# Three 16-wide attentions as one packed, one-pass score program, with the clip moved to the exponentials

## The chip, the cores and the metric

One core of a Trainium2 chip runs the whole kernel in one launch. The metric is the device time of that launch in microseconds (us). TensorE is called PE in the rows, VectorE DVE, ScalarE ACT, GpSimd POOL and SyncE SP.

## The reference

Eight residual blocks act on `x` (8 batches × 256 rows × 256); each takes a layernorm of `x` and adds its result times tanh of a gate. The context is 8 × 256 × 192. Three blocks matter here; each has 16 heads of width 16.

```python
# l1x: cross attention; masked query rows attend evenly
attn = jnp.einsum('bhnd,bhmd->bhnm', q * scale, k)
attn = jnp.where(pad_mask[:, None, :, None], attn, jnp.float32(-1000000000.0))
out = jnp.einsum('bhnm,bhmd->bhnd', softmax(attn), v)
# l3x: cross attention with biases, clip and projection
attn = jnp.einsum('bhqd,bhkd->bhqk', q, k) * scale
attn = jnp.clip(attn, -CLAMP, CLAMP)                       # CLAMP = 10000.0
x = jnp.einsum('bhqk,bhkd->bqhd', softmax(attn), v).reshape(B, Nq, Cq)
return x @ Wo + bo
# l3f: self attention; 5 register rows, the others split in pos and ~pos
l = jnp.where(key_mask[:, None, None, :], logits, -jnp.inf)   # registers + same side
reg_out = (x_pos[:, :REG] + x_neg[:, :REG]) * 0.5
tok_out = jnp.where(pos[:, :, None, None], x_pos[:, REG:], x_neg[:, REG:])
return out @ W_proj + b_proj
```

The other blocks are a similarity (l0x), a feed-forward block (l0f), two mixtures of experts (l1f, l2f) and an attention with heads of width 64 (l2x).

## The kernel before

The blocks run one behind the other with a barrier of semaphores (`phase`) between them. Each engine has its own instruction stream, written out in Python; the order in which the code emits instructions is the order on the engine, and engines meet through semaphores alone. Nothing reorders them.

Two programs compute 16-wide heads.

**Packed** (class `Packed`, function `packing` for each engine) serves l1x. GpSimd splits q, k, the layernormed x and the context into a high part in the fp32r format and a low part (`parts`: a cast, L717, and a subtraction, L719). Products run as three one-pass products of parts (`mm3`, L1736 to L1738). SyncE copies the parts of q and k by DMA (`rows_of`, L563) into `qpack` and `kpack`, so that 48 rows hold (high, low, high) of q against (high, high, low) of k for one head: a single pass of 48 rows then gives the score with little loss. A head needs two sets of scores: queries × keys (L2091), of which VectorE takes the negated maximum (`maximum`, L1163), and keys × queries (L2105) with two more rows that add the negated maximum. VectorE splits the maxima (`maxima`), PE transposes them (L2074), ScalarE copies them out and SyncE writes them to `qpack`. ScalarE's exponential (L1629) then writes the probabilities already transposed, and PE multiplies them with the values of four heads at a time (`values`, L2120). A column of ones beside the values gives the sum.

In loop round n, PE does the first scores of batch n+1 beside the transposed ones of batch n, since these use different halves of the rows; between heads stand the transposes and products that prepare batch n+2 and finish batch n−1. PSUM has eight banks: two for scores, two for transposed scores, two for probabilities × values, and two "rooms" (banks 6 and 7) that everything else takes in turn (`place`). VectorE's round: the maxima, the mask multiply at head 4, both halves of the outputs at head 8.

**Attn** serves l2x, l3x and l3f. Heads of 16 are padded to 32 columns and scored in fp32 (L1898). In l3x VectorE clips every score (L1042) and takes the maximum (L1044); ScalarE's exponential has the maximum as a bias. PE transposes the probabilities (L1915), ScalarE (l3x) or VectorE (l3f) copies them out of PSUM, PE multiplies with the values (L1939) and projects (`finish`: transposes L1982, products L1987). The loop over batches is a hardware loop in which the projections stand between two batches. GpSimd does one root a batch (L700). l3f also scores 80 register queries (5 rows × 16 heads) and keeps pos and neg apart by two mask rows in q and k.

## Time and profile before

| what | us |
|---|---|
| three timed runs, median (lowest to highest) | 3416.39 (3400.31 to 3434.22) |
| profiled execution, its span | 3390.0 |
| l1x, from 263.4 to 538.0 | 274.6 |
| l3x, from 2334.5 to 2799.0 | 464.5 |
| l3f, from 2870.3 to 3382.0 | 511.7 |

For the profiled execution only its span is given: the time from its first to its last instruction. The stages' limits are the barriers between blocks, read from the timeline. Times of instructions below come from that one execution.

### The profile page before, as it was taken

The page shows a single profiled execution, that of the slowest core. Times are in us where ns is not written, and L with a number is a line of the kernel's source. Part 1 is how long each engine was busy: PE and PEld are TensorE (multiplying, and loading weights), DVE is VectorE, ACT ScalarE, POOL GpSimd, SP SyncE. Part 2 cuts the span into 40 slices and gives each one's busy share as a digit, 9 for nine tenths or more (in the row PEclk, how much of TensorE's full clock was granted, in tenths as well). Part 3 has the DMA queues.
Part 4 walks back from the last instruction along what each step waited for, and adds up shares of the span by engine and source line. Part 5 has one row for each costly group of instructions (what it writes and reads, how often), then busy time and mean ns, then how long its engine had stood idle before and what let it go on. Part 6 is the DMA issues. An engine that isn't in the chain of part 4 may idle for free.

```text
span 3390.0 us, 37402 instructions
## 1 busy us (share of the span) xinstructions
PE 2575.8 (76%) x13142; PEld 1918.9 (57%) x13142; DVE 1580.7 (47%) x2934; ACT 872.7 (26%) x2012; POOL 785.2 (23%) x709
## 2 busy tenths in 40 slices
PE   3795885487887728888888577673888884999998
PEld 3574554376666625555556466552555653766665
DVE  3443566256657423333334533224564554454454
ACT  1221342111111103323333112122453451232232
POOL 3103223334334133333434422213000000000000
PEclk8795676699898868888989588786896996988899
DMA  3704441122232230000000013321000000000000
GB/s 115 253 0 57 56 60 54 68 96 98 78 103 91 83 118 5 2 2 2 2 2 0 13 50 95 105 86 55 5 3 2 5 1 0 1 0 0 0 0 25
DMA packets 91147, 151.93 MB, mean 45 GB/s; under 512 B 7612, under 2 KB 75900, under 8 KB 88428
## 3 DMA queue, kind: packets, MB, share of 16 engines
q1 hardware_dynamic: 61820, 101.93, 11.1%
q0 software_dynamic: 8736, 27.76, 2.6%
q10 hardware_dynamic: 20496, 20.97, 1.7%
q8 instruction: 59, 0.97, 0.1%
q14 instruction: 36, 0.29, 0.0%
HBM read 90.51 MB, written 47.19 MB: 41 GB/s over the span
## 4 chain that ended last, share of the span: by engine, by line
PE 57%; issue 20%; DVE 10%; POOL 5%; DMA 3%; ACT 3%; SPq 1%; another core or an unknown queue 1%; ACTq 0%; DVEq 0%; POOLq 0%
PE bank L1898 11%; PE bank L1853 7%; PE bank L1736 6%; PE bank L1915 6%; PE bank L1737 5%; PE bank L1738 5%; PE bank L1939 4%; PE bank L1873 2%; DMA arena<-rows_by_expert 2%; POOL arena L786 2%; DVE nmax L1044 1%; PE bank L1987 1%; DVE split L1332 1%; PE bank L2091 1%; ACT arena L1457 1%
## 5 line engine op out<-in xcount | busy, mean ns | idle before, releaser
L1898 PE MATMUL bank<-arena 64*128 64x256 f32 x1536 | 472.4, 442 | 6.2 <-ACT arena L1457 6.2
L1898 PEld LDWEIGHTS bank<-arena 64*128 64x128 f32 x1536 | 283.0, 207 | 141.6 <-issue 108.5
L1542 ACT ACTIVATE arena<-bank,nmax 128x256 f32<-128x256 f32 x512 | 226.3, 470 | 459.8 <-DVE nmax L1044 457.8
L1915 PE MATMUL bank<-ident,arena 128*128 128x128 f32 x1536 | 272.0, 306 | 74.7 <-POOL arena L829 44.2
L1044 DVE TENSOR_REDUCE nmax<-bank 128x2 f32<-128x512 f32 x256 | 175.8, 690 | 321.0 <-PE bank L1898 316.9
L1457 ACT ACTIVATE arena<-bank 128x512 f32<-128x512 f32 (+1 forms) x346 | 198.2, 580 | 463.1 <-PE bank L1853 112.0
L1736 PE MATMUL bank<-split,ewl 128*128 128x512 f32 x514 | 227.3, 442 | 98.8 <-DVE arena L1329 86.2
L1915 PEld LDWEIGHTS bank<-ident,arena 128*128 128x128 f32 x1536 | 177.6, 151 | 210.1 <-issue 112.2
L700 POOL TENSOR_TENSOR rstd<-rstd,mhalf 128x2 f32<-128x2 f32 x40 | 28.0, 700 | 996.8 <-DVE rstd L972 839.2
L1329 DVE TENSOR_TENSOR arena<-sil,bank 128x512 f32<-128x512 f32 x136 | 93.2, 685 | 315.9 <-ACT sil L1670 300.3
L1737 PE MATMUL bank<-split,ewh 128*128 128x512 f32 x514 | 217.2, 423 | 0.0
L1738 PE MATMUL bank<-split,ewh 128*128 128x512 f32 x514 | 215.5, 419 | 0.0
L1333 DVE TENSOR_TENSOR split<-arena,split 128x512 fp32r<-128x512 f32 x136 | 211.9, 1558 | 4.7
L759 POOL CAST ewh<-ew 128x1536 fp32r<-128x1536 f32 (+1 forms) x47 | 91.6, 1948 | 500.0 <-DMA ew<-in_we 500.0
L761 POOL TENSOR_TENSOR ewl<-ew,ewh 128x1536 fp32r<-128x1536 f32 (+1 forms) x47 | 204.2, 4344 | 3.8
L1054 DVE COPY arena<-bank 128x512 f32<-128x512 f32 (+1 forms) x264 | 177.1, 674 | 55.7 <-PE bank L1915 55.6
L1670 ACT ACTIVATE sil<-bank 128x512 f32<-128x512 f32 x136 | 81.4, 598 | 440.5 <-PE bank L1738 413.6
L1736 PEld LDWEIGHTS bank<-split,ewl 128*128 128x128 f32 x514 | 107.9, 210 | 131.5 <-DVE arena L1329 71.5
L1736 PE MATMUL bank<-ewh,split 128*128 128x256 f32 x544 | 167.8, 309 | 17.7 <-DVE split L1333 10.0
L1939 PE MATMUL bank<-arena 128*17 128x256 f32 (+1 forms) x1536 | 157.3, 423 | 24.2 <-ACT arena L1457 16.6
L825 POOL TENSOR_TENSOR esum<-esum,minus 128x2 f32<-128x2 f32 x128 | 89.8, 702 | 326.8 <-ACT arena L1542 326.7
L1737 PE MATMUL bank<-ewl,split 128*128 128x256 f32 x544 | 155.8, 286 | 0.0
(394 smaller groups left out, 4764.7 us busy)
## 6 DMA issues: line engine op xcount, KB each, us to landing
ew<-in_we SPq DMA_DIRECT2D x32, 768.0 KB, 8.0
ew<-in_we SPq DMA_DIRECT2D x15, 1408.0 KB, 6.1
rows_by_expert<-mrow ACTq DMA_DIRECT2D x1, 20480.0 KB, 58.2
arena<-rows_by_expert SPq DMA_DIRECT2D x23, 512.0 KB, 6.5
rows_by_expert<-arena SPq DMA_DIRECT2D x38, 256.0 KB, 5.4
ct<-in_ctxT SPq DMA_DIRECT2D x32, 192.0 KB, 2.4
kpack<-khl SPq DMA_DIRECT2D x48, 128.0 KB, 4.4
qpack<-qhl SPq DMA_DIRECT2D x48, 128.0 KB, 5.8
```

What stands on the lines that cost most here:

```text
L761: nc.gpsimd.tensor_tensor(low, whole, high, ALU.subtract).then_inc(m["ws"], 1)
L1044: V.tensor_reduce(nmax[:, h, :], src.rearrange("p (t k) -> p t k", t=T), AXX, ALU.max, negate=True).then_inc(m["mx"], 1)
L1333: tt(lo, whole, hi, ALU.subtract).then_inc(m["hid"], 1)
L1457: return A(dst, src, ACT.Copy)
L1542: ins = A(prob[h % 3][:, t * S:(t + 1) * S], src[:, t * S:(t + 1) * S], ACT.Exp, bias=nmax[:, h, t:t + 1], **kw)
L1736: mm(out_, al, bh, start=start, stop=False)
L1737: mm(out_, ah, bl, start=False, stop=False)
L1738: return mm(out_, ah, bh, start=False, stop=stop)
L1853: ins = mm(dst, w[:, c, gr * P:(gr + 1) * P], of[:, c, :], start=c == 0, stop=c == kt_ - 1 and not s.split)
L1898: ins = mm(bank[h % 3][:, t * S:(t + 1) * S], q[r0:r0 + 64, gr, t * P:(t + 1) * P], kT[r0:r0 + 64, gr, :], start=True, stop=True)
L1915: ins = tr(bank[3 + k % 2][:, c0:c0 + P], prob[k % 3][:, t * S + kt * P:t * S + (kt + 1) * P], ident[:, :])
L1939: ins = mm(bank[5 + gr // 2 % 2][r0:r0 + s.vs, gr % 2 * S:(gr % 2 + 1) * S], v[:, kt, h * s.vs:(h + 1) * s.vs], probT[h % 8][:, kt * S:(kt ...
```

## The change

l3x and l3f become `Packed` stages like l1x, and the program itself is rewritten for all three.

- Run-ahead of three batches in place of two, loop from n = −3; three rooms (banks 5, 6, 7) in place of two, and one bank (4) for probabilities × values. The order of users is a new table in `Packed`.
- The products for the next batch, 12 in a row before, are halves of 6 behind separate heads: queries at heads 7 and 8, keys at 10 and 11, values at 14 and 15. Both halves of the outputs, at head 8 on VectorE before, stand at heads 5 and 7.
- Clip in l3x: the negated maxima are clamped (two small instructions for each half of the heads), and the 128x512 exponentials of every head are clamped between e^−27 and e^60: heads with even number by GpSimd, odd ones by VectorE. `values` waits for both.
- Biases of v and of the projection become one row (`bot`), which GpSimd adds to x ahead of time (`with_bias`); the projection is four fp32 products per batch (eight instructions) and one VectorE instruction of 128x512 (`finish`).
- l3f has two mask rows more in each pack (24 loads a round, in place of 12 for l1x and l3x), and takes mean and root from the similarity stage before it. Its register rows are eight small products, two transposes, two products with 272 columns and a selection.
- GpSimd fills `kpack` with ones (three memsets of 2048 columns at the start of l1x and l3x, in place of six small DMAs), and splits the weights of l3x and l3f at the end of l2f.

```diff
+        for n in range(-3, B + 1):
+            for what, at, here in (("rs", n, own), ("m1", n, True), ("xT", n + 3, True), ("z0", n - 1, True),
+                                   ("rt", n, own), ("z1", n - 1, True), ("rg", n - 1, own), ("q", n + 3, True),
+                                   ("m0", n + 1, True), ("k", n + 3, True), ("ro", n, own), ("w", n - 1, proj),
+                                   ("v", n + 3, True), ("y", n - 1, proj)):
+                if here and 0 <= at < B:
+                    b = sum(self.used) % ROOMS
                     self.place[what, at] = b, self.used[b]
                     self.used[b] += 1
...
+L2X = Attn("l2x", 64, 0.125)
+L3X = Packed("l3x", 0.25, bias=True, clip=True, proj=True)
+L3F = Packed("l3f", 0.25, proj=True, own=True)
...
+                for n in range(-3, B):
+                    ahead = 0 <= n + 2 < B
+                    if ahead:
+                        if n >= 1:
+                            sp.wait_ge(m["st"], at["st"] + n * NH)
+                        if n == -2:
+                            sp.wait_ge(m["ones"], at["ones"] + s.total["ones"])
+                            if s.own:
+                                sp.wait_ge(m["mc"], 1)
+                        sp.wait_ge(m["qs"], at["qs"] + 2 * n + 6)
+                        rows_of(qpack[(n + 2) % 3], qhl, 0, (0, 1, 0), m["pq"])
                     if 0 <= n:
                         maxima(n, 1)
-                    if n + 2 < B:
-                        if n >= 1:
-                            sp.wait_ge(m["st"], s.base["st"] + n * NH)
-                        sp.wait_ge(m["ks"], s.base["ks"] + 2 * n + 6)
-                        rows_of(kpack[(n + 2) % 3], khl, (0, 0, 1), m[f"pl{(n + 2) % 3}"])
-                        sp.wait_ge(m["qs"], s.base["qs"] + 2 * n + 6)
-                        rows_of(qpack[(n + 2) % 3], qhl, (0, 1, 0), m[f"pl{(n + 2) % 3}"])
+                    if ahead:
+                        rows_of(qpack[(n + 2) % 3], qhl, 1, (0, 1, 0), m["pq"])
+                        if s.own:
+                            for j in range(2):
+                                masks_of(n + 2, qpack[(n + 2) % 3], j, 0, m["pq"])
+                        sp.wait_ge(m["ks"], at["ks"] + 2 * n + 6)
+                        for j in range(2):
+                            rows_of(kpack[(n + 2) % 3], khl, j, (0, 0, 1), m["pk"])
+                        if s.own:
+                            for j in range(2):
+                                masks_of(n + 2, kpack[(n + 2) % 3], j, 2, m["pk"])
                     if 0 <= n + 1 < B:
                         maxima(n + 1, 0)
+                    if not s.own and n + 4 < B:
+                        context(n + 4)
...
+                def clamp(n, h):
+                    i = n * NH + h
+                    pool.wait_ge(m["e"], at["e"] + i + 1)
+                    w = pT16[i % 8][:, :]
+                    nc.gpsimd.tensor_scalar(w, w, math.exp(EXP_HIGH), math.exp(EXP_LOW), ALU.min, ALU.max)\
+                        .then_inc(m["cl"], 1)
...
+                for n in range(-3, B + 1):
+                    ahead = 0 <= n + 3 < B
+                    if ahead and not s.own:
                         context(n + 3)
-                    if n + 3 < B:
-                        root(m, n + 4, rstd[:, :], rstd[:, :], mhalf[:, 0:T])
+                    for h in range(NH):
+                        if s.clip and 0 <= n < B and by_pool(h + 1) > by_pool(h):
+                            clamp(n, h)
+                        if h == 4 and ahead:
+                            filled("xT", n + 3)
+                            parts(xT16, xt[:, :, :], "xs", n + 3)
+                        if h == 9 and ahead:
+                            filled("q", n + 3)
+                            if n + 3 > 0:
+                                pool.wait_ge(m["pq"], at["pq"] + s.loads * (n + 3))
+                            parts(qhl, qf[:, :, :], "qs", n + 3)
+                        if h == 10 and n + 4 < B and not s.own:
+                            root({"asked": asked[s.name]}, n + 5, rstd[:, :], rstd[:, :], mhalf[:, 0:T])
+                        if h == 12 and ahead:
+                            filled("k", n + 3)
+                            if n + 3 > 0:
+                                pool.wait_ge(m["pk"], at["pk"] + s.loads * (n + 3))
+                            parts(khl, kf[:, :, :], "ks", n + 3)
+                        if h == 13 and s.proj and n + 4 < B:
+                            with_bias(n + 4)
 
...
+                    if s.clip:
+                        ch.link(ts(nmf[:, c, :, :, :], nmf[:, c, :, :, :], -CLAMP / s.qscale, EXP_HIGH / s.qscale,
+                                   ALU.max, ALU.add))
+                        ch.link(ts(nmf[:, c, :, :, :], nmf[:, c, :, :, :], (CLAMP + EXP_LOW) / s.qscale, None, ALU.min))
...
+                def clamp(n, h):
+                    i = n * NH + h
+                    dve.wait_ge(m["e"], at["e"] + i + 1)
+                    w = pT16[i % 8][:, :]
+                    ts(w, w, math.exp(EXP_HIGH), math.exp(EXP_LOW), ALU.min, ALU.max).then_inc(m["cv"], 1)
...
+                for n in range(-3, B + 2):
                     for h in range(NH):
+                        if h == 0 and s.proj and 0 <= n - 2 < B:
+                            finish(n - 2)
                         if 0 <= n + 1 < B:
                             maximum(n + 1, h)
                             if h == 7:
                                 maxima(n + 1, 0)
                             if h == NH - 1:
                                 maxima(n + 1, 1)
-                        if h == 4 and n + 2 < B:
-                            queries(n + 2)
-                        if n == B and h < B - 1:
-                            for t in range(T):
-                                b, k = s.place[f"z{t}", h]
-                                dve.wait_ge(m[f"mf{b}"], k + 1)
+                        if s.clip and 0 <= n < B and by_pool(h + 1) == by_pool(h):
+                            clamp(n, h)
+                        if h == 1 and s.own and 0 <= n < B:
+                            register_maximum(n)
+                        if h in (5, 7) and 0 <= n - 1 < B:
+                            outputs(n - 1, h // 2 - 2)
+                        if h == 8 and s.own and 0 <= n - 1 < B:
+                            with_registers(n - 1)
+                        if h == 9 and s.mask and 0 <= n + 3 < B:
+                            queries(n + 3)
+                        if h == 10 and n + 4 < B and not s.own:
+                            statistics(n + 4)
+                        if h == 12 and s.own and 0 <= n < B:
+                            register_outputs(n)
+                        if h == 13 and n + 4 < B:
+                            normal(n + 4)
+                        if n == B and h < B - 1 and not s.own:
+                            filled(last, h)
                             stats_of(h)
-                        if h == 8 and 0 <= n - 1 < B:
-                            outputs(n - 1)
-                        if h == 10 and n + 3 < B:
-                            statistics(n + 3)
-                        if h == 13 and n + 3 < B:
-                            normal(n + 3)
...
+                    if s.clip:
+                        k = by_pool(gr * 4 + 4)
+                        pe.wait_ge(m["cl"], at["cl"] + n * by_pool(NH) + k)
+                        pe.wait_ge(m["cv"], at["cv"] + n * (NH - by_pool(NH)) + gr * 4 + 4 - k)
...
+                for n in range(-3, B + 1):
+                    ahead = 0 <= n + 3 < B
+                    behind = 0 <= n - 1 < B
                     for h in range(NH):
                         heads_of(n, h)
-                        if h == 0 and n + 2 < B:
-                            turned(n + 2)
-                            keys(n + 2)
-                        if h == 1:
-                            if 0 <= n - 1:
-                                values(n - 1, 3)
-                            if n + 2 < B:
-                                values_of(n + 2)
+                        if h == 0 and s.own and 0 <= n < B:
+                            register_scores(n)
+                        if h == 1 and behind:
+                            values(n - 1, 3)
                         if h == 2 and 0 <= n < B:
                             maxima(n, 1)
-                        if h == 3 and n + 2 < B:
-                            queries(n + 2)
+                        if h == 3 and ahead:
+                            turned(n + 3)
+                        if h == 4 and behind:
+                            outputs(n - 1, 0)
                         if h in (5, 9, 13) and 0 <= n < B:
                             values(n, h // 4 - 1)
-                        if h in (6, 7) and 0 <= n - 1:
-                            outputs(n - 1, h - 6)
+                        if h == 5 and s.own and 0 <= n < B:
+                            register_turned(n)
+                        if h == 6 and behind:
+                            outputs(n - 1, 1)
+                        if h == 6 and s.own and behind:
+                            registers(n - 1)
+                        if h in (7, 8) and ahead:
+                            queries(n + 3, h - 7)
                         if h == 9 and 0 <= n + 1 < B:
                             maxima(n + 1, 0)
+                        if h in (10, 11) and ahead:
+                            keys(n + 3, h - 10)
+                        if h == 11 and s.own and 0 <= n < B:
+                            register_values(n)
+                        if h == 12 and s.proj and behind:
+                            outputs_turned(n - 1)
+                        if h in (14, 15) and ahead:
+                            values_of(n + 3, h - 14)
+                        if h == 15 and s.proj and behind:
+                            finish(n - 1)
```

On PE in l1x, ahead of the products for the coming queries, before (`bank` is a PSUM bank, `xT,wqs` are those products, `ident,nmhl` the transposed maxima):

```order
L2105 MATMUL bank<-qpack,kpack 128x256 x2
L2074 MATMUL bank<-ident,nmhl 16x128 x2
L2091 MATMUL bank<-kpack,qpack 128x256 x2
L2105 MATMUL bank<-qpack,kpack 128x256 x2
L1736 MATMUL bank<-xT,wqs 128x256
L1737 MATMUL bank<-xT,wqs 128x256
L1738 MATMUL bank<-xT,wqs 128x256
```

(and so on to 12 products) and after:

```order
L2037 MATMUL bank<-kpack,qpack 128x256 x2
L2051 MATMUL bank<-qpack,kpack 128x256 x2
L1760 MATMUL bank<-xT,wqs 128x256
L1761 MATMUL bank<-xT,wqs 128x256
L1762 MATMUL bank<-xT,wqs 128x256
L1760 MATMUL bank<-xT,wqs 128x256
L1761 MATMUL bank<-xT,wqs 128x256
L1762 MATMUL bank<-xT,wqs 128x256
L2037 MATMUL bank<-kpack,qpack 128x256 x2
L2051 MATMUL bank<-qpack,kpack 128x256 x2
```

The 12 products in a row became two runs of six, each behind a head's pair of scores, and stand at another place of the round.

On VectorE in l3x, from one head to the next, before (clip, then maximum):

```order
L1042 TENSOR_SCALAR sil<-bank 128x512
L189 REGISTER_ALU
L1044 TENSOR_REDUCE nmax<-sil 128x2
L1033 REGISTER_ALU
L1041 REGISTER_ALU
L1042 TENSOR_SCALAR sil<-bank 128x512
```

and after (`nmf` are the maxima, `pT` the exponentials):

```order
L1117 TENSOR_REDUCE nmf<-bank 128x2 x2
L1161 TENSOR_SCALAR pT_5<-pT_5 128x512
L1117 TENSOR_REDUCE nmf<-bank 128x2 x2
L1125 TENSOR_SCALAR nmf<-nmf 128x16
L1127 TENSOR_SCALAR nmf<-nmf 128x16
L1129 CAST nmhl<-nmf 128x2x4 x2
L1132 TENSOR_TENSOR nmhl<-nmf,nmhl 128x2x4 x2
L1161 TENSOR_SCALAR pT_7<-pT_7 128x512
L1117 TENSOR_REDUCE nmf<-bank 128x2 x2
L1161 TENSOR_SCALAR pT_1<-pT_1 128x512
```

The clip of the scores left the way between the score and its maximum; a clamp of an exponential stands between every second pair of maxima, and the small clamps (L1125, L1127) stand ahead of the split of the maxima.

On GpSimd in l3x, which before had one root a batch (L700) and nothing else, one round's second half after:

```order
L765 TENSOR_SCALAR pT_6<-pT_6 128x512
L765 TENSOR_SCALAR pT_0<-pT_0 128x512
L735 CAST qhl<-qf 128x512
L737 TENSOR_TENSOR qhl<-qf,qhl 128x512
L765 TENSOR_SCALAR pT_2<-pT_2 128x512
L704 TENSOR_TENSOR rstd<-rstd,mhalf 128x2
L765 TENSOR_SCALAR pT_4<-pT_4 128x512
L735 CAST khl<-kf 128x512
L737 TENSOR_TENSOR khl<-kf,khl 128x512
L758 TENSOR_TENSOR x<-x,bot 128x512
L765 TENSOR_SCALAR pT_6<-pT_6 128x512
```

Clamps alternate with conversions of q and k, and each waits in this order.

## Rows read from the trace of the kernel before

**Rows 1.** First line of the page.

```profile
span 3390.0 us, 37402 instructions
```

**Rows 2.** Windows by stage: window, us, PE, PEld, DVE, ACT, POOL busy, PEclk, DMA, GB/s.

```profile
263.40:538.00 274.60, 204.76 (x1440) 139.82 (x1440) 140.15 (x321) 96.52 (x184) 65.37 (x72) 0.69 0.41 54
...
2334.50:2799.00 464.50, 392.66 (x2048) 266.33 (x2048) 254.39 (x493) 209.00 (x457) 5.61 (x8) 0.87 0.01 4
...
2870.30:3382.00 511.70, 472.63 (x2560) 335.57 (x2560) 257.63 (x549) 144.74 (x337) 5.61 (x8) 0.88 0.00 0
```

**Rows 3.** Groups and timeline, l3x: scores, clip, one batch's projection.

```profile
L1898 PE MATMUL bank<-arena 64*128 64x256 f32 x512 | 153.9, 429 | 0.0
...
L1042 DVE TENSOR_SCALAR sil<-bank 128x512 f32<-128x512 f32 x88 | 60.7, 689 | 50.7 <-PE bank L1898 50.3 <-issue 0.2
...
2794.95 2.92 PE L1987 MATMUL bank<-wo_l3x,oT 128*128 128x256 f32 x8
```

**Rows 4.** Timeline of PE in l1x: start, us, instruction, wait before it.

```profile
348.66 1.11 PE L2041 MATMUL bank<-ident,xn 128*128 128x128 f32 x4
...
372.43 0.58 PE L2091 MATMUL bank<-kpack,qpack 48*128 48x256 f32 x1 [0.34 <-DVE nmf L1163]
...
373.03 0.57 PE L2091 MATMUL bank<-kpack,qpack 48*128 48x256 f32 x1
...
379.82 1.11 PE L2041 MATMUL bank<-ident,xn 128*128 128x128 f32 x4
...
380.94 0.41 PE L1737 MATMUL bank<-cT,wks 96*128 96x256 f32 x1
...
383.08 0.41 PE L1738 MATMUL bank<-cT,wks 96*128 96x256 f32 x1
...
384.15 1.91 PE L2120 MATMUL bank<-pT,v 128*17 128x256 f32 x16
...
388.13 0.39 PE L2091 MATMUL bank<-kpack,qpack 48*128 48x256 f32 x1
...
388.57 0.39 PE L2074 MATMUL bank<-ident,nmhl 128*16 128x128 f32 x2
...
394.55 1.06 PE L2120 MATMUL bank<-pT,v 128*17 128x256 f32 x16
```

**Rows 5.** Small windows in l1x (two) and in l3f, columns as in 2.

```profile
387.60:391.00 3.40, 1.87 (x17) 1.21 (x15) 1.39 (x2) 2.28 (x5) 0.00 (x0) 0.94 0.01 2
...
404.60:408.00 3.40, 2.38 (x20) 0.99 (x20) 2.86 (x8) 1.19 (x3) 0.70 (x1) 0.50 0.58 102
...
3090.60:3094.00 3.40, 3.40 (x10) 1.88 (x8) 2.29 (x7) 0.84 (x2) 0.00 (x0) 0.50 0.00 0
```

**Rows 6.** Waits, l1x rounds: waiter, releaser: idle us, times, longest.

```profile
PE bank L2074 <- DVE x L890: 11.0, 6, 2.3
...
PE bank L1736 <- ACT v L1457: 9.0, 6, 1.5
```

**Rows 7.** Instructions of two DVE lines: ns min/median/max, first and last start.

```profile
L1163 DVE TENSOR_REDUCE nmf<-bank x128: 675/686/694, 295.9 to 517.3; 128x2 f32<-128x512 f32 x128
...
L1332 DVE CAST split<-arena x136: 424/426/2798, 662.3 to 2278.9; 128x512 fp32r<-128x512 f32 x121, 64x512 fp32r<-64x512 f32 x15
```

**Rows 8.** POOL lines in l1x (the last two groups: timeline, memset).

```profile
L717 POOL CAST khl<-kf x8: 611/611/612, 278.0 to 477.6; 128x512 fp32r<-128x512 f32 x8
...
L719 POOL TENSOR_TENSOR khl<-kf,khl x8: 1265/1270/1295, 278.7 to 478.3; 128x512 fp32r<-128x512 f32 x8
...
270.12 0.61 POOL L717 CAST cT<-ct 96x512 fp32r<-96x512 f32 x1 [10.63 <-DMA ct<-in_ctxT]
...
L606 POOL MEMSET mrow<- 128x512 f32 x1 | 0.5, 526 | 0.0
```

**Rows 9.** SyncE's loads: issue of one set (timeline), and landing (page, 6).

```profile
392.40 3.81 SPq L563 DMA_DIRECT2D kpack<-khl  x6
...
qpack<-qhl SPq DMA_DIRECT2D x48, 128.0 KB, 5.8
```

More of the change, by code:

```diff
@@ new lines, in registers @@
+                def registers(n):
+                    act.wait_ge(m["pq"], at["pq"] + s.loads * (n + 1))
+                    if n == 0:
+                        act.wait_ge(m["qi"], 3)
+                    else:
+                        made("rs", n - 1)
+                    for j in range(2):
+                        to = qx[64 * j:64 * j + 48, :].rearrange("p (r c) -> p r c", c=NX + 2)[:, :, 0:NX]
+                        copy(to.rearrange("p r (g k) -> p r g k", k=NH)[:, :, :, j],
+                             qpack[n % 3][64 * j:64 * j + 48, :, 0:NREG]).then_inc(m["rx"], 1)
```

1084 lines of the change are left out of this document (491 added, 593 removed).

## The prediction

> **What bounds the kernel now.** I read the windows by stage first, then instruction groups, then the PE timeline of one batch, then the waits. The run shown in the profile spans 3390.0 us [rows 1]; the median of the three timed runs is 26.4 us above it, and I add that at the end. A measurement of this kernel can tell about 1% from no change. The three attentions that the change touches take 274.6, 464.5 and 511.7 us, together 1250.8 [rows 2]; the other five stages, 2139 us, keep their instructions, and I leave them alone.
>
> The windows show PE busy in 85% of l3x and 92% of l3f at a granted clock of 0.87 and 0.88 [rows 2]: these two are bound by TensorE's fp32 work. In l3x the scores alone are 512 instructions of 429 ns, 153.9 us busy, and VectorE adds a clip pass of 689 ns for each head [rows 3]. l1x does the same attention (without projection) in 274.6 us with 1440 matmuls. It has another limit: PE is busy 75% of it at a granted clock of 0.69, DVE 51% [rows 2]. From its first maximum at 295.9 to its last at 517.3 [rows 7] lie eight rounds, 27.7 us each, with 32.5 us ahead of them and 20.7 behind; a full round takes 31.2 us, from one block of four transposes to the next (348.66 to 379.82) [rows 4].
>
> What a round of l1x is made of [rows 4]: at the lower level (clock 0.50, 1.2 GHz) an unhindered head, two scores beside two transposed scores, takes 0.60 us (372.43 to 373.03); a product 0.214 us (ten intervals from 380.94 to 383.08); a block of 16 P·V products 1.91; four transposes 1.11. At 2.4 GHz a head takes 0.44 (388.13 to 388.57) and a P·V block 1.06. I halve the product to 0.115 and the transposes to 0.55. A round has 16 heads, 36 products, 4 blocks, three sets of four transposes and four small transposes: 7.0 + 4.1 + 4.2 + 1.7 + 0.6 = 17.6 us at 2.4 GHz, and 9.6 + 7.7 + 7.6 + 3.3 + 0.8 = 29.0 at 1.2. VectorE needs 17.5 (140.15 by 8) [rows 2]. So PE and VectorE have the same work if the clock is high, and PE alone is the limit if it is low. The small windows show both levels: 0.94 in one 3.4 us stretch with steady products, 0.50 in another where PE had gaps; and a stretch of l3f that PE fills wholly is at 0.50 as well [rows 5], so full work alone doesn't secure the clock.
>
> **The change, part by part.**
>
> *l1x.* The two repeated stalls are the transposes of the maxima, which wait 11.0 us in 6 times for VectorE, and products that wait 9.0 us in 6 times for ScalarE's copy out of the only free room [rows 6]. The first arises because VectorE does both halves of the outputs at head 8, right behind the maxima; now they stand at heads 5 and 7. The second arises in blocks of 12 products through two rooms; now they are halves of 6 through three. I take both as gone, 3.3 us a round: 31.2 becomes 27.9. Behind them the next limit is that a head's maximum takes 0.69 us on VectorE [rows 7] against 0.44 to 0.60 on PE, so a head without other PE work costs 0.69, and one with 6 products or a block costs PE's sum. Over a round that head-by-head maximum is about 21.4 us at 2.4 GHz. I take a mean clock of 0.80 (l1x has 0.69 now, the fp32 stages 0.88 [rows 2]): 17.6 / 0.8 = 22, and 2 for leftover waits: 24 us. Ahead of the rounds nothing is won: the chain transposes, products, split, loads, scores is as before. The products' order puts the queries first, and GpSimd's three memsets of 2048 columns (a 512 column one takes 0.53 [rows 8], so about 6.3 us together) fall into the 10.6 us that it waits for the context now [rows 8]. Stage: 32 + 8 × 24 + 19.5 = 243.5, that is −31.
>
> *l3x.* Out go the fp32 scores, the clip of 512 columns a head, the transposes of probabilities and their copies, and the projections that stand between batches. In comes a round like that of l1x with four transposes and eight projection instructions (a batch's eight take 2.92 us [rows 3]): PE 17.6 + 0.55 + 2.9 = 21 at 2.4 GHz, about 34 at 1.2. VectorE: 17.5 less the mask multiply (0.69) and the two additions to x (0.96), plus 8 clamps of the exponentials at 0.69 [rows 3], 0.8 for four small clamps of the maxima, 0.75 for the end: 23 us. ScalarE has 12 us a round in l1x (96.52 by 8 [rows 2]) and gets some copies more, some 15 us, hidden. GpSimd: four conversions at 0.61 + 1.27 [rows 8], one addition of 1.3, a root of 0.7, and 8 clamps. The trace of before has no clamp there; the one-input cast gives 0.61 and the two-input subtraction 1.27 for 512 columns, so 14.4 to 19.7 us a round, beside the rest. I take the lower end (one input, one output), and neither end is on the path. `values` must wait for the clamps of its four heads; they are queued on GpSimd behind a conversion of 1.88 at most, and the next block of values is four heads behind, about 6 us, so the wait is covered. A round: PE at clock 0.80 needs 26.3, VectorE 23, and they interleave by head; with 3.2 for waits at the clamps I take 29.5. Stage: 36 ahead (l1x's 32.5, plus the memsets and bias work, here in front of the first root with nothing to cover it), 23 for the first round, which has no exponentials, 7 × 29.5, and 27 for the last round, projection and statistics: 292.5, that is −172.
>
> Of GpSimd beside VectorE the trace shows this: a VectorE cast that takes 424 ns at its median took 2798 ns once [rows 7]. The Trainium skill says (Advanced Engine Details and Errata, VectorE Performance Modes) that VectorE's second port to SBUF is shared with GpSimd, so that the fast forms and GpSimd's instructions keep each other out. That speaks against splitting a clamp between those two. By it the 14.4 to 19.7 us of GpSimd would be added in part to VectorE's 23: it is a cause for rival E below, and the maxima read PSUM, which I take to go on.
>
> *l3f.* The same round with the registers' part: eight small fp32 products, two transposes, two products of 272 columns, one selection, together 2.8 us, and no clamps: PE 17.6 + 3.5 + 2.8 = 23.9 at 2.4 GHz, about 38.5 at 1.2. VectorE stays near 17 (no mask multiply, no statistics). PE is the limit, so its clock would be as in the present l3f, 0.88: 27 us. SyncE issues 24 loads a round for q, k and mask rows. Six of the present loads take 3.81 us to issue, 0.64 to 0.76 each, and land 5.8 us later [rows 9]; at 0.74 that is 17.8 us of queue a round, below 27 and off the path, as they are made for two rounds later. Stage: 26 (statistics and root exist already), 24, 7 × 27, 28: 267, that is −245. The new splits of weights on GpSimd stand in l2f ahead of a long wait there and cost nothing that I can see; without this cover they would be 2 × 5.7 us (three casts, three subtractions each).
>
> **Sum.** −31 − 172 − 245 = −448: the span becomes 2942, the time 2968 us.
>
> **The rivals.**
>
> B, *the clock stays low*. For it: l1x, the only stage of this form, has 0.69 [rows 2], and its stalls are what the program keeps in part (VectorE 0.69 a head against PE 0.60). Against: l3f's PE is filled. If all three run at 1.2 GHz, rounds are 29.5, 34 and 38.5: 287.5 + 334 + 360.5 = 982, that is −269; span 3121, time 3147.
>
> C, *no stall is left and the clock is high*: rounds of 20, 25 and 24.5. For it: three rooms and a run-ahead of three. Stages 211.5 + 255 + 244.5 = 711: span 2850, time 2877.
>
> E, *the clamps are dear*: either GpSimd needs far more than 1.27 for 512 columns, or it and VectorE hold each other up. GpSimd's other work is 9.5 us, so it decides once a clamp takes above 2.5 us: (29.5 − 9.5) / 8. At 4 us a round of l3x is 41.5: 7 × 12 = +84, span 3026, time 3052. Exclusion without a dear clamp gives 37.6 to 42.9 a round (23 + 14.4 to 19.7), which is the same size.
>
> D, *slower than before: the loads become serial with the round*. q and k rows for a batch are released by GpSimd and pushed by one queue, and if the three buffers turn out one too few, each round would be PE at 1.2 GHz, then the conversion (1.9), the issue (12 × 0.74 or 24 × 0.74) and the landing (5.8 [rows 9]): 45.6, 50.6 and 63.5 us. Stages 416, 450 and 535: +151, span 3541, time 3567. It decides from a mean round of 46 us in the three stages. Against: in l1x the same loads are hidden, PE's waits name VectorE and ScalarE [rows 6], not DMA.
>
> That the change doesn't do what it says would show as matmul forms of fp32 64-row scores remaining in l3x; the instruction order excludes it, so no chance.
>
> **How the numbers follow.** My forecast 0.55, B 0.22, E 0.11, C 0.10, D 0.02. The predicted time is that of the likeliest, 2968. Without D the cases reach from 2877 to 3147; the ends of the unknown costs (three stages' heads and tails, some ±10) go beside C. The range is 2860 to 3140, which leaves out D and the upper half of B. All cases but D are over 1% faster: faster 0.97, same 0.01, slower 0.02.
>
> **What would show it.** Right: stage windows near 243, 292 and 267; mean clocks near 0.8 in l1x and l3x and 0.88 in l3f; the two waits [rows 6] gone from the list of waits; rounds of 24, 29.5 and 27 from one block of transposes to the next. The clamp of GpSimd at 0.6 to 1.3 us. Wrong: clocks of 0.5 to 0.7 (B); `values` in l3x released by GpSimd or VectorE's clamp for more than 3 us a round (E); PE released by the loads of qpack or kpack (D). The largest single risk is the clock, since the same sum of PE work makes 22 or 29 us in l1x by it.

## The result and the profile after

The changed kernel takes 2852.5 us (median of four runs, 2838.2 to 2860.3) against 3424.3 for the kernel before (four runs): 0.835 of it, with a 95% interval of 0.830 to 0.840. That is 572 us less, and 7.5 us under the low end of the range. The first line of the page and the windows by stage of the kernel after (columns as in [rows 2]: PE, PEld, DVE, ACT, POOL busy, then PEclk) answer to [rows 1, 2]:

```profile
span 2836.5 us, 32922 instructions
...
264.00:482.90 218.90, 186.32 (x1440) 122.05 (x1440) 144.40 (x323) 96.85 (x184) 70.90 (x75) 0.77 0.48 67
...
2270.70:2514.70 244.00, 198.29 (x1540) 133.91 (x1540) 171.28 (x409) 110.09 (x217) 122.00 (x150) 0.83 0.43 60
...
2587.50:2828.50 241.00, 215.43 (x1696) 146.55 (x1696) 135.50 (x298) 115.82 (x234) 55.19 (x56) 0.88 0.36 57
```

l1x, l3x and l3f went from 274.6, 464.5 and 511.7 us to 218.9, 244.0 and 241.0: −546.9 of the 553.5 by which the span fell. The other 6.6 lie in the rest, whose instructions are as before but for the new splits of weights on GpSimd at the end of l2f (465.0 us before, 458.6 after). The stages' mean clocks, 0.77, 0.83 and 0.88, are close to the 0.80, 0.80 and 0.88 of the prediction, yet the stages are 25, 48 and 26 us shorter than it said. The windows of single rounds show why. They are, in order, for l1x its first round with scores, one full round and its tail; for l3x a full round; for l3f its first round and a full one.

```profile
297.90:323.50 25.60, 22.85 (x90) 16.88 (x90) 16.58 (x35) 3.74 (x7) 11.41 (x13) 0.52 0.53 73
...
362.40:381.60 19.20, 18.67 (x182) 12.29 (x180) 17.40 (x39) 12.02 (x24) 8.21 (x9) 1.00 0.66 96
...
454.20:482.90 28.70, 22.23 (x130) 11.21 (x128) 9.78 (x33) 10.74 (x20) 0.00 (x0) 0.50 0.01 2
...
2384.00:2405.80 21.80, 20.99 (x194) 14.14 (x192) 20.43 (x49) 13.53 (x29) 14.65 (x18) 1.00 0.56 84
...
2619.20:2646.50 27.30, 25.00 (x100) 18.89 (x99) 15.16 (x32) 6.61 (x13) 9.31 (x9) 0.50 0.41 57
...
2691.40:2715.30 23.90, 23.88 (x213) 16.03 (x209) 17.82 (x38) 14.21 (x31) 6.89 (x7) 1.00 0.47 72
```

These full rounds have the clock at 1.00 and PE busy 96 to 100% of them; they take 19.2, 21.8 and 23.9 us. The low level stands in parts of the stages' heads, in each first round (that of l3x takes 25.9 us at 0.56), in part of the round behind it, and in the tail of l1x (the third line). A stage's mean mixes the two.

The full rounds of l3x don't always run at 1.00. A second profile of the same kernel, unedited, has l1x at 219.0 us and l3f at 241.0 as here, but l3x at 255.6; two of its rounds, the slowest and the one that is like the first profile's:

```profile
2366.50:2396.50 30.00, 28.01 (x195) 18.11 (x193) 22.58 (x48) 13.73 (x27) 14.47 (x19) 0.73 0.40 61
...
2421.50:2444.00 22.50, 21.04 (x195) 14.14 (x193) 20.84 (x49) 13.56 (x29) 14.39 (x18) 1.00 0.58 82
```

Over all profiles below in which l3x has no edit (seven with these two) the stage takes 243.4 to 263.9 us, and single rounds up to 31.7 us at a clock of 0.63; nothing here shows what brings the clock down there. An unedited l1x takes 212.0 to 219.0 us (four profiles) and an unedited l3f 240.8 to 242.4 (eight). An experiment's stage is read against these spreads.

The clamps, and VectorE's cast beside them (the same line as the second one of [rows 7]):

```profile
L765 POOL TENSOR_SCALAR pT<-pT x64: 605/615/640, 2334.1 to 2500.3; 128x512 f32<-128x512 f32 x64
...
L1161 DVE TENSOR_SCALAR pT<-pT x64: 408/426/839, 2334.5 to 2500.7; 128x512 f32<-128x512 f32 x64
...
L1352 DVE CAST split<-arena x136: 423/426/5702, 605.3 to 2214.9; 128x512 fp32r<-128x512 f32 x121, 64x512 fp32r<-64x512 f32 x15
```

GpSimd's clamp takes 0.615 us, as taken; VectorE's 0.426 and not 0.689, since it reads and writes SBUF, where the clip of [rows 3] read PSUM. The Trainium skill has this difference (Advanced Engine Details and Errata, VectorE Performance Modes: the two-port mode needs source and destination in SBUF), and the trace agrees: 0.426 us against 0.689 for the same 512 columns.

### The profile page after: what moved, and what is told of

Its sections match the earlier page's. It is cut to its first block, busy times and chain, and to the rows that moved or that the text cites. A ratio compares the mean times of both kernels' runs of the same rounds, so it can differ in the third digit from the quotient of the medians.

```text
span 2836.5 us, 32922 instructions
## 1 busy us (share of the span) xinstructions
PE 2101.5 (74%) x11770; PEld 1574.5 (56%) x11770; DVE 1379.2 (49%) x2599; ACT 745.2 (26%) x1669; POOL 967.4 (34%) x900
## 4 chain that ended last, share of the span: by engine, by line
PE 53%; issue 21%; DVE 11%; POOL 5%; DMA 5%; SPq 2%; ACT 2%; another core or an unknown queue 1%; DVEq 0%; POOLq 0%; ACTq 0%
PE bank L1760 8%; PE bank L1761 6%; PE bank L1762 6%; PE bank L2037 5%; PE bank L1886 5%; PE bank L1863 4%; PE bank L2071 3%; DMA arena<-rows_by_expert 3%; PE bank L1899 3%; PE bank L1914 2%; PE bank L1876 2%; DVE split L1352 2%; DVE nmf L1117 2%; PE bank L2226 1%; DVE x L1378 1%
## 5 line engine op out<-in xcount | busy, mean ns | idle before, releaser
L1117 DVE TENSOR_REDUCE nmf<-bank 128x2 f32<-128x512 f32 x384 | 256.3, 687 | 124.3 <-PE bank L2037 122.1
L1609 ACT ACTIVATE pT<-bank 128x512 f32<-128x512 f32 x384 | 225.6, 596 | 218.8 <-PE bank L2051 217.2
L2037 PE MATMUL bank<-kpack,qpack 48*128 48x256 f32 (+1 forms) x768 | 199.2, 360 | 29.2 <-DVE nmf L1117 15.4
L1037 DVE TENSOR_REDUCE nmax<-bank 128x2 f32<-128x512 f32 x128 | 87.6, 690 | 232.9 <-PE bank L1886 229.6
L2051 PE MATMUL bank<-qpack,kpack 50*128 50x256 f32 (+1 forms) x768 | 192.5, 351 | 4.1 <-ACT pT L1609 4.1
L2037 PEld LDWEIGHTS bank<-kpack,qpack 48*128 48x128 f32 (+1 forms) x768 | 125.0, 213 | 114.8 <-DVE nmf L1117 53.8
L1760 PE MATMUL bank<-ewh,split 128*128 128x256 f32 x544 | 168.2, 309 | 24.9 <-DVE split L1353 15.7
L1539 ACT ACTIVATE arena<-bank,nmax 128x256 f32<-128x256 f32 x256 | 119.0, 470 | 247.5 <-DVE nmax L1037 245.4
L1473 ACT ACTIVATE arena<-bank 128x512 f32<-128x512 f32 x154 | 91.9, 597 | 312.7 <-PE bank L1863 111.9
L1886 PE MATMUL bank<-arena 64*128 64x256 f32 x512 | 155.6, 447 | 6.2 <-ACT arena L1473 6.2
L1762 PE MATMUL bank<-ewh,split 128*128 128x256 f32 x544 | 155.6, 286 | 0.0
```

What stands on the lines that cost most here:

```text
L1117: V.tensor_reduce(nmf[:, c, :, j, r], bank[h % 2][:, :].rearrange("p (t k) -> p t k", t=T), AXX, ALU.max, negate=True).then_inc(m["mx"], 1)
L1539: ins = A(prob[h % 3][:, t * S:(t + 1) * S], bank[h % 3][:, t * S:(t + 1) * S], ACT.Exp, bias=nmax[:, h, t:t + 1], accum_out=esum[:, h, t: ...
L1609: A(pT16[i % 8][:, :], bank[2 + h % 2][:, :], ACT.Exp, scale=s.qscale).then_inc(m["e"], 1)
L1760: mm(out_, al, bh, start=start, stop=False)
L1762: return mm(out_, ah, bh, start=False, stop=stop)
L1886: ins = mm(bank[h % 3][:, t * S:(t + 1) * S], qT[r0:r0 + 64, gr, t * P:(t + 1) * P], kT[r0:r0 + 64, gr, :], start=True, stop=True)
```

## The experiments

All of them are the changed kernel with one edit. Its own time, in a later group of runs, was 2852.0 us (six runs, 2828 to 2864), so times below are read against 2852. They come from four groups of runs, in which the kernel before took 3404, 3418, 3396 and 3380 us; so a difference from 2852 of less than some 1% is told apart only within a group, or by a stage's window. "Rounds" are full rounds, from one block of four transposes to the next.

**1. Products 12 in a row, everywhere.**

```diff
-                        if h in (7, 8) and ahead:
-                            queries(n + 3, h - 7)
+                        if h == 8 and ahead:
+                            queries(n + 3, 0)
+                            queries(n + 3, 1)
```

(and so for keys, behind head 11, and values, behind 15)

> The changed kernel with the products again 12 in a row (queries behind head 8, keys behind 11, values behind 15), rest as changed. Theory S (stalls of PE pull the granted clock down, and the changed rounds run at 1.00 because nothing stalls PE): a run of 12 products keeps PE busy, but VectorE gets no score for 1.4 us and a later head waits for it; rounds of l1x stay at 19 to 20 us and clock 1.00, time 2850 to 2870. Rival L (the long blocks were what held the clock and the round back): l1x rounds 22 us or more, time 2900 or more.

Measured: 2840.7 us, some 10 under the range. l1x 18.7 a round, l3f 22.7, both at clock 1.00. Long blocks aren't what cost l1x its time, and l3f gains by them (its stage 230.9 us, where 240.8 is the shortest without the edit). l3x had rounds of 24.4 to 28.4 at 0.74 to 0.91 and a stage of 259.8 us; that is inside the 243.4 to 263.9 of unedited ones, so a cost there isn't shown by it. What points to one is experiment 4: its one long-block round of l3x at 1.00 took 24.0 us, where unedited ones at 1.00 take 21.8 to 23.2.

**2. The outputs of VectorE at head 8 in l1x and l3x.**

```diff
-                        if h in (5, 7) and 0 <= n - 1 < B:
+                        if h in (5, 7) and s.own and 0 <= n - 1 < B:
                             outputs(n - 1, h // 2 - 2)
+                        if h == 8 and not s.own and 0 <= n - 1 < B:
+                            outputs(n - 1, 0)
+                            outputs(n - 1, 1)
```

> In l1x and l3x both halves of the outputs stand again at head 8 of VectorE's round, right behind the maxima, rest as changed (l3f untouched). Theory S: PE stalls about 2 us a round for the maxima's transposes, the clock leaves 1.00, a round loses more than the stall: l1x from 19.2 to 22 or more, l3x likewise, time 2890 to 2920. Rival N (a stall costs its own length and the clock is set by something else): 7 x 2 x 1.8 = +25 at most, clock 1.00 in the rounds, time 2865 to 2880.

Measured: 2855.7 us, under both ranges, and a split answer. In l1x rounds rose to 24.2 us at a clock of 0.79 and the stage to 231.1 us, 12 over the longest without the edit, which the total hides in its spread; l3x (247.0 us) had 25.5 us at 0.84 and 0.89 in its first two and 22.2 and 22.4 at 1.00 in its last two, as unedited ones have too. One of l1x's rounds:

```profile
365.40:389.60 24.20, 23.10 (x182) 14.76 (x180) 16.36 (x38) 12.11 (x24) 8.27 (x9) 0.79 0.53 77
```

PE's idle time in it is only 1.1 us; its busy time rose from 18.7 to 23.1 with the same 182 matmuls. So of the 5 us 4.4 are the clock.

**3. Two rooms.** `ROOMS = 3` became `ROOMS = 2`.

> Two rooms (banks 5 and 6) in place of three for all that passes through PSUM between heads, rest as changed. Theory S: each product block waits for ScalarE's copy out of the room before it, some 1 to 1.5 us a round in all three stages, and the clock falls with it: rounds +3 us, time 2910 or more. Rival N: the halves leave a head or two between users of a room, so two rooms are enough: time within 10 us of 2852.

Measured: 2895.2 us, +43, which neither side had expected: l3f alone pays. It took 278.8 us in place of 241.0, with rounds of 31.8 to 32.9; l3x 257.1, inside the spread of unedited ones; l1x 219.0, unchanged. A round of l3f:

```profile
2718.00:2750.90 32.90, 27.16 (x209) 17.88 (x209) 16.08 (x37) 14.39 (x30) 6.95 (x7) 0.90 0.33 52
```

The registers' chain (scores, turned, values, selection) passes through the rooms as well. In these rounds PE waits some 6 us each, and the waits name readers of a room: VectorE's outputs and ScalarE's copies of values, keys and registers. That is why l3f needs the third. In l1x two rooms are enough, as rival N has it.

**4. Edits 1 and 2 together.**

> Both together: 12 products in a row, and both halves of the outputs at head 8 in l1x and l3x. With three rooms and run-ahead of three left, this is the old order of a round. Theory S: l1x rounds of 23 to 27 us, clock 0.7 to 0.85 in them, time 2910 to 2960. Rival N: no more than the sum of the two stalls, time 2885 at most. A third, R (the three rooms and the run-ahead did it, not the order): time within 15 us of 2852.

Measured: 2838.0 us, which is where R has it. l1x 19.2 a round at 1.00. The late outputs cost 0.5 us a round here (18.7 in experiment 1) and leave the clock alone, though PE is idle 1.4 us of a round, more than the 1.1 of experiment 2 at 0.79. A wait of this size may or may not bring the clock down; which of the two isn't told by its length. That its place in the round decides is a guess.

**5. l1x alone in its old order** on all engines, with three rooms and the run-ahead of three kept. On PE:

```diff
+                        if s.mask:
+                            if h == 0 and ahead:
+                                turned(n + 3)
+                                keys(n + 3, 0)
+                                keys(n + 3, 1)
+                            if h == 1 and behind:
+                                values(n - 1, 3)
+                            if h == 1 and ahead:
+                                values_of(n + 3, 0)
...
+                            if h == 3 and ahead:
+                                queries(n + 3, 0)
```

> The changed kernel, but l1x alone with its old order of a round on all engines (transposes and 12 keys behind head 0, values behind 1, queries behind 3, outputs behind 6 and 7, both outputs of VectorE at head 8, the mask multiply at head 4), with three rooms and the run-ahead of three kept; l3x and l3f as changed. Open after the first four: what took l1x from 31.2 to 19.2 us a round. Theory O (the order: blocks of 4 transposes and 24 products behind two heads starve VectorE, then the maxima come late, and the clock falls): l1x rounds of 25 to 31 us at a clock of 0.65 to 0.8, stage 255 to 275, time 2885 to 2910. Rival R (run-ahead and rooms): rounds of 19 to 21, time 2840 to 2865.

Measured: 2917.1 us, l1x 285.4 us, rounds of 32.4 to 33.5, above both ranges. But the waits show a delay that the edit itself made:

```profile
POOL khl L739 <- DMA kpack<-khl: 61.0, 3, 20.9
...
DVE xn L1134 <- POOL rstd L708: 23.4, 3, 7.9
```

SyncE issued the k rows late in the round, GpSimd's conversion waited up to 20.9 us for them, and the root behind it on GpSimd's queue held VectorE 7.8 us a round. Hence two more runs.

**6. The same with k rows issued first**, as the old program did.

```diff
+                        if s.mask:
+                            sp.wait_ge(m["ks"], at["ks"] + 2 * n + 6)
+                            for j in range(2):
+                                rows_of(kpack[(n + 2) % 3], khl, j, (0, 0, 1), m["pk"])
```

> The run with the old order in l1x once more, with k rows issued ahead of the q rows in each round of l1x, so that GpSimd's k conversion no longer waits for them for most of a round. If the old order itself (12 products behind heads 0, 1 and 3, late outputs) keeps PE stalling: l1x rounds of 24 to 30 us at a clock of 0.65 to 0.8, stage 250 to 270, time 2880 to 2900. If only the late loads did it: rounds of 19 to 20, time 2840 to 2860, and then the run-ahead of three is what the changed kernel gains in l1x.

Measured: 2870.7 us (2846 to 2882), l1x 259.2 us, rounds of 24.5 to 27.9: stage and rounds as the side of the order has them, the time under its 2880 to 2900. In the group of this run and the next the stage l2f, which no edit touches, took 435 us in place of 459 to 464, so the stage of l1x is what is compared, not the total. PE is idle 3 to 5 us a round here, and its clock is 0.71 to 0.77.

**7. The same with early outputs.** PE's outputs at heads 4 and 6, VectorE's at 5 and 7.

> As the one before, with the outputs of PE at heads 4 and 6 and of VectorE at heads 5 and 7 as in the changed kernel; the products stay behind heads 0, 1 and 3. If the late outputs stall PE and the clock follows: l1x back at 19 to 21 us a round and a clock near 1.00, time 2840 to 2860. If the product blocks in the first four heads do it: rounds stay within 1 us of the run before.

Measured: 2867.1 us (its profiled execution, 2875.0, is one of the longer of four from 2830.9 to 2879.1; the totals of this run and the one before overlap and tell nothing), l1x 267.5 us, rounds of 26.4 to 27.9 at 0.74 to 0.76:

```profile
382.20:410.10 27.90, 24.08 (x182) 16.04 (x181) 16.77 (x40) 12.07 (x23) 8.16 (x9) 0.74 0.46 66
```

So the late outputs weren't it: in the old order l1x stays at 24 to 28 us a round whatever the outputs do. Of the 12 us between 31.2 and 19.2 a round, some 7 are the order of a round. The edit moves PE's transposes and products behind heads 0, 1 and 3, but also the conversions on GpSimd, the copies on ScalarE, the mask multiply and the order of the rooms; these runs don't tell which of them it is. The other 5 belong to the rest (run-ahead, loads, rooms), which they don't take apart either, apart from that two rooms alone cost l1x nothing.

**8. A stall of known length.** Fills of 128x512 on VectorE behind head 8, five a round in l1x, ten in l3f.

```diff
+                        if h == 8 and not s.clip and 0 <= n - 1 < B:
+                            for _ in range(10 if s.own else 5):
+                                ch.link(V.memset(scr[:, 512:1024], 0.0))
```

> The changed kernel with idle work on VectorE behind the outputs of head 8: five fills of 512 columns a round in l1x, ten in l3f (0.2 to 0.5 us each, so 1 to 2.5 and 2 to 5 us a round that delay the next maxima), l3x as changed. Theory S (a stall of PE in each round brings the granted clock down, and the round loses more than the stall): in l1x rounds rise from 19.2 by 3 us or more with a clock of 0.75 to 0.9; in l3f, which has 6 us a round more on PE than on VectorE, by 2 to 8 us. Rival N (the clock does not follow stalls; the old order of l1x lost its time by waiting alone): l1x rises by the fills' own length, clock 1.00 in the full rounds.

Measured: 2925.3 us. The fills' row, and a round of each stage:

```profile
L1227 DVE MEMSET scr<- x120: 485/485/485, 350.7 to 2914.3; 128x512 f32 x120
```

```profile
370.00:399.20 29.20, 26.28 (x182) 16.30 (x180) 19.14 (x43) 12.40 (x24) 8.17 (x9) 0.68 0.45 63
...
2741.70:2772.20 30.50, 25.64 (x210) 17.18 (x208) 21.54 (x48) 14.16 (x31) 7.03 (x7) 0.89 0.36 56
```

With the wait between two of them (18.0 us for 104) a fill costs 0.66 us: 3.3 us a round in l1x, 6.6 in l3f. l1x's rounds rose by 10 us, three times that: 7.6 of them are PE's own work at a clock of 0.68, 2.4 are idle time. l3f's rose by 6.6, at 0.89. No pause of PE in these rounds of l1x is longer than 2.2 us. This is the clearest evidence for the mechanism, since l1x without an edit has 1.00 in its last three rounds in each of four profiles: 3.3 us more on VectorE, which had 17.4 us a round, make some 21, so by the sums alone a round would rise by 2 us; it rises by 10, most of it by the clock, which fell below the 0.75 to 0.9 expected. That it is the balance of the two engines that makes l1x pay three times and l3f once is argued from two stages and not shown.

**9 and 10. All clamps on GpSimd; all on VectorE.** `by_pool(h)` returns `h` or `0`.

> All 16 clamps of the exponentials of l3x on GpSimd, none on VectorE, rest as changed. GpSimd then has 9.5 + 16 x 0.615 = 19.4 us a round, VectorE 20.8 - 3.4 = 17.4, PE 21. Theory P (PE's sum is the limit of a full round, each clamp engine has slack): rounds stay 22 to 23 us, time within 10 us of 2845. Rival Q (clamps of heads in a row queue on GpSimd behind conversions of 1.9 us, so the values wait): rounds 24 or more and a clock below 1.00, time 2870 or more.

> All 16 clamps of l3x on VectorE, none on GpSimd. VectorE then has 20.8 + 8 x 0.426 = 24.2 us a round, over PE's 21. If VectorE's sum is the limit: rounds of 24.5 to 25 us, and PE's waits bring the clock to 0.8 to 0.9, time 2865 to 2880. If the two engines' shared way to SBUF cost much in the changed kernel, taking the clamps off GpSimd gives part back: VectorE's sum under 23 and rounds of 22 to 23, time 2850 or less.

Measured: 2837.7 us (2833 to 2843) and 2862.5 (2847 to 2866), in one group; l3x 246.0 and 265.3 us. Unedited ones have 243.4 to 263.9, so it is the 25 us between the two, with ranges that don't touch, that carries the reading. A full round of each:

```profile
2400.00:2422.40 22.40, 20.99 (x194) 14.22 (x192) 18.62 (x41) 13.51 (x28) 18.69 (x27) 1.00 0.56 82
```

```profile
2399.90:2428.60 28.70, 27.93 (x195) 18.13 (x193) 23.30 (x56) 13.46 (x27) 10.19 (x10) 0.73 0.44 64
```

GpSimd can take all 16 at no cost; on VectorE alone the sum passes PE's, and three of four rounds have a clock of 0.68 to 0.73, so that PE is busy 97% again, with slower work. They take 27.7 to 29.6 us and not the 24.5 to 25 expected, since the clock falls as well.

GpSimd and VectorE do hold each other up, as the trace of the changed kernel shows in l3x (first VectorE, then GpSimd):

```profile
2400.57 1.20 DVE L1127 TENSOR_SCALAR nmf<-nmf 128x16 f32<-128x16 f32 x1
...
2400.46 1.27 POOL L758 TENSOR_TENSOR x<-x,bot 128x512 f32<-128x512 f32 x1
```

VectorE's small clamp, 0.174 us in its median, starts 0.1 us behind GpSimd's addition and ends with it. Its four small clamps take 2.3 us in the next round, and 0.7 unhindered. With all clamps on GpSimd the median of this one is 0.543 us; with all on VectorE single large clamps take up to 1.54 us behind a conversion. Against the unhindered lengths it is some 2 to 3 us of VectorE's busy time a round either way; where GpSimd has all the clamps it doesn't show in the stage's time.

**11. Work that nobody reads, to raise the clock early.** 24 products ahead of the first transposes, 12 behind the first two sets, 20 ahead of the first scores and 4 behind each head of the first round.

```diff
+                        if n == -1 and h == 0:
+                            warm(20)
                         heads_of(n, h)
+                        if n == -1:
+                            warm(4)
```

> The changed kernel plus products on PE whose result nobody reads, in its idle time ahead of the full rounds of all three stages: 24 before the first transposes, 12 behind each of the first two sets, 20 before the first scores and 4 behind each head of the first round. If the first round (25.6, 25.9 and 27.3 us at a clock of 0.50 to 0.56) is long because of the low clock after PE's idle head: it falls to the 17 to 20 us of VectorE's maxima at a clock of 0.9 or more, 6 to 8 us a stage, time 2825 to 2835. If the clock stays low whatever fills the gaps: the extra products cost 0.2 us each at the low level, +8 us a stage, time 2870 or more.

Measured: 2848.4 us, between the two ranges. The first rounds of l1x and l3f:

```profile
301.40:322.30 20.90, 20.36 (x135) 16.17 (x133) 14.21 (x33) 3.63 (x7) 8.22 (x9) 1.00 0.54 72
2628.20:2657.10 28.90, 28.67 (x143) 22.82 (x141) 12.02 (x27) 6.04 (x11) 6.92 (x7) 0.70 0.18 27
```

The clock came up in l1x and l3x (20.9 us at 1.00 there too), and the round fell by 5 us; l3f's did not, its stage took 249.1 us against 241.0, and the total is the same.

**12. fp32 in place of the one pass.** The packed rows of both score products read as fp32.

```diff
-                            ins = mm(bank[h % 2][:, t * S:(t + 1) * S], q[rows, r, t * P:(t + 1) * P], k[rows, r, :],
+                            ins = mm(bank[h % 2][:, t * S:(t + 1) * S], q[rows, r, t * P:(t + 1) * P].bitcast(F32), k[rows, r, :].bitcast(F32),
                                      start=True, stop=True)
```

> The changed kernel with the same 48 to 52 packed rows multiplied as fp32 in place of one-pass fp32r, in both sets of scores of all three stages. If the single pass is what makes l3x and l3f short: a head's scores cost up to four times 0.44 us at 2.4 GHz, +21 us a round in all three stages at most, and less as far as the two row halves still run beside each other; rounds of 36 to 43 us, time 3200 to 3350. If the schedule and not the pass is what matters, VectorE's 17 to 21 us a round hide it and the time is under 3000.

Measured: 3070.7 us (one execution), +218, between the two ranges. A round of l1x:

```profile
371.20:399.90 28.70, 28.70 (x246) 19.29 (x244) 17.87 (x38) 12.28 (x23) 8.26 (x9) 1.00 0.44 64
```

9.5 us more than 19.2; l3x has 31.1 and l3f 34.0, 9 and 10 more, less than half of the 21 expected at most. The two row halves still run beside each other: their products start 0.01 to 0.02 us apart. So some 218 of the 572 us hang on the single pass; the rest of the gain stands even with fp32 scores, in a program without a clip ahead of the maximum, without transposed probabilities and their copies, and with projections between heads instead of between batches.

**13. Long blocks in l1x and l3f, halves in l3x** (each where experiment 1 found it better).

> The changed kernel with the products in runs of 12 in l1x and l3f (one run behind heads 8, 11 and 15) and in halves of 6 in l3x. The first experiment showed l3f rounds of 22.7 in place of 23.8, l1x rounds of 18.7 in place of 19.2, and l3x rounds of 26.4 in place of 23: if these are separate, l1x and l3f give 3 + 10 us and l3x stays at 244: 2838, that is 12 to 16 us under the unchanged one on the same chip. If what l1x and l3f gained was the chance of the clock's level in the first rounds, it is within 5 us of it.

Measured beside the unchanged one: 2836.3 us (six runs, 2828 to 2842) against 2852.0 (2828 to 2864); ratios to the kernel before 0.834 (0.829 to 0.839) and 0.837 (0.831 to 0.843), whose intervals overlap. In the profiles l3f has 233.3 us against 241.0 and l1x 215.5 against 219.0. It is the best version by its median, some 0.5%, which these runs don't separate from none; l3f's 8 to 10 us are seen in each of three kernels with the edit, while l1x's 215.5 lies inside the 212.0 to 219.0 of stages without it.

## Why the prediction was right and where it failed

**Right.** Direction and size class of all three stages; the sums of PE's work, 17.6, 21 and 23.9 us a round at 2.4 GHz against 18.7, 21.0 and 23.9 measured; that l1x would gain from the order of its round; GpSimd's clamp; loads off the path (rival D never appeared); the weights' splits under cover in l2f. Of the two stalls of [rows 6] none is left. The cause that I named for the first, the late outputs, is only a part: experiment 2 shows 5 us a round for them in the new order, experiment 4 0.5 with long blocks, and experiment 7 nothing in the old order, which keeps its 24 to 28 us.

**The step that failed** is the divisor in each round: "17.6 / 0.8", "PE at clock 0.80 needs 26.3", and "its clock would be as in the present l3f, 0.88". I read the mean clock of a stage and used it for a round. The full rounds run at 1.00, and the measured rounds of 19.2, 21.8 to 23.2 and 23.9 us are those of rival C (20, 25, 24.5), to which I gave 0.10. The fine windows [rows 5] showed two levels and not a mean, but I misread them: the stretch at 0.94, which I called one of steady products, has PE busy 1.87 of 3.40 us, less than the 2.38 of the one at 0.50. And the trace of before could not have told the level for l3f: its rounds have PE busy 93 to 95% and a clock of 0.80 to 0.94. So C was a case to be weighed higher, not one that the rows proved; and that l3x too came out at C in the first profile is in part luck, since the second has a round of 30 us at 0.73, the prediction's 29.5. In terms of the sum, rounds gave back 36 us in l1x and 54 in l3x against the forecast (first maximum to the end of the last: 156.3 and 175.6 us against 192 and 229.5), and 31 in l3f.

**Mis-sized terms beside it.** VectorE's clamp (0.426 against 0.689, 2 us a round). Heads and tails were longer than I said: l1x 33.9 + 28.7 against 32 + 19.5, since its tail runs at 0.50, where that of the kernel before had 0.82; l3x 38.9 + 29.5 against 36 + 27; l3f's head 31.8 against 26. The 21.4 us of the head-by-head maximum are about 18 if the prediction's own terms are added by head; the forecast didn't use them. And the 26.4 us that I added from span to median are 16.0 here.

**The range** ended at 2860. It took rival C's time, 2877, and 17 us for heads and tails. From C's 2877 to the measured 2852.5 it is 10.4 us of the offset (26.4 in place of 16.0), 7.1 in the three stages, and 6.6 in the rest. The offset alone is more than the 7.5 us by which the time falls outside.

## What to carry to other kernels

Don't multiply work by a mean clock: cut a stage into rounds, read the clock of each, and work out the round at either level; both sums are cases of the forecast. In l1x, where two engines are nearly equally loaded, 3.3 us more on VectorE cost three times their length, through the clock; in l3f, where PE alone is the limit, 6.6 us cost their own length. Long product blocks gained 8 to 10 us in l3f, where VectorE has slack. Take a second profile of the same kernel before reading a stage's difference: l3x alone moves by 20 us without an edit.

## What the runs showed of the hardware

PE at full work doesn't raise its clock at once: the first round of l3f had 25.0 us busy in 27.3 at 0.50, before the full rounds came to 1.00. In experiment 11 it had 28.67 us busy in 28.90 at 0.70. Work that nobody reads raised the clock in two stages and not in the third. The clock also falls without a long pause: to 0.68 in the rounds of experiment 8, where no pause of PE is longer than 2.2 us.

An instruction of VectorE on SBUF that starts behind one of GpSimd can be held until that one ends: the small clamp above, and VectorE's cast of 424 ns, which [rows 7] shows at 2.8 us. The prediction says once; that is its longest, and 26 of the 136 took over 0.9 us, all beside GpSimd's splits of weights. In the kernel after, three took 5.7 us, each begun behind a subtraction of GpSimd and done 0.3 us after it. The large clamps of VectorE beside GpSimd's, both in SBUF, stayed at 426 ns in the median and 839 at most. The trace agrees with the rule of the Trainium skill that the prediction weighed (Advanced Engine Details and Errata, VectorE Performance Modes, on the shared port), and in this kernel it doesn't show in the time: the run with most work on GpSimd is the shortest of its group.
